# Causal attention: where the mask of the row maxima is added, which of two engines pays for it, and when the next stage's weights are loaded

## The reference

```python
# layer 0, attention, 16 heads of 16: x = x + attn(layernorm(x))
q, k, v = (jnp.einsum('bte,hed->bhtd', x, W) for W in (Wq, Wk, Wv))
scores = jnp.where(causal, jnp.einsum('bhtd,bhsd->bhts', q, k), -jnp.inf) / sqrt(E)
out = jnp.einsum('bhts,bhsd->bhtd', jax.nn.softmax(scores, axis=-1), v)
# layer 0, ffn: x = x + mlp(n) + experts(n), n = layernorm(x)
# top-k over product keys, 1024 experts (Wq, keys, down_embed, up_embed), and a gated MLP (Wg, Wu, Wd)
# layer 1: rotary attention and a mixture of experts, not touched
```

## Time and profile before

| | |
|---|---|
| time, median of 3 runs | 4173.62 us (4170.66 to 4175.27) |
| profiled execution: its own time | 4178.98 us |
| profiled execution: span | 4177.1 us |
| causal attention | from the start to about 1165 us |
| steps with m units | up to about 1120 us |
| PE busy in the span | 3942.8 us (94%) |
| DVE busy in the span | 2784.8 us (67%) |
| ACT busy in the span | 2640.7 us (63%) |

### The profile page before, as it was taken

One profiled execution on the slowest core, in us unless ns is written; L12 is line 12 of the kernel. 1 busy time (PEld: TensorE's weight loads), 2 busy tenths in 40 slices (PEclk: granted clock), 3 DMA queues, 4 the chain that ended last, 5 costly groups with the idle time before them and its releaser, 6 DMA issues. The chain is left out here.

```text
span 4177.1 us, 65914 instructions
## 1 busy us (share of the span) xinstructions
PE 3942.8 (94%) x23476; PEld 2362.2 (57%) x23476; DVE 2784.8 (67%) x5635; ACT 2640.7 (63%) x3262; POOL 1554.6 (37%) x1303
## 2 busy tenths in 40 slices
PE   7999999999968999999999989997999999999999
PEld 4455445554447788787887855554444444444444
DVE  7888778887668878878788545445545555554553
ACT  2566666666765545545455334444888888888888
POOL 3222222222334534435344211111555455455545
PEclk7999999999989999999999999999999999999999
DMA  7553444344142232332323210004666766667674
GB/s 180 129 113 75 103 99 104 91 112 111 29 121 76 61 106 77 80 103 61 109 74 84 84 35 1 1 1 106 154 154 154 163 146 154 154 148 159 148 160 99
DMA packets 205761, 429.98 MB, mean 103 GB/s; under 512 B 47584, under 2 KB 72560, under 8 KB 189056
## 3 DMA queue, kind: packets, MB, share of 16 engines
q1 hardware_dynamic: 193360, 411.56, 41.1%
q0 software_dynamic: 4160, 6.35, 0.6%
q10 hardware_dynamic: 7920, 7.87, 0.6%
HBM read 338.59 MB, written 87.03 MB: 102 GB/s over the span
## 5 line engine op out<-in xcount | busy, mean ns | idle before, releaser
L2202 ACT ACTIVATE gelu_out<-hidden,b_col 128x1024 f32<-128x1024 f32 x1024 | 1054.4, 1117 | 181.7 <-PE hidden L2125 176.0
L2185 POOL TENSOR_TENSOR combined<-combined,gated 128x512 f32<-128x512 f32 x480 | 621.5, 1295 | 647.4 <-DVE gated L2302 471.2
L663 DVE TENSOR_REDUCE maxima<-front_and_scoresT 128x1 f32<-128x512 f32 (+3 forms) x1280 | 725.6, 628 | 97.2 <-PE front_and_scoresT L471 61.7
L563 ACT ACTIVATE probsT<-front_and_scoresT 128x1024 f32<-128x1024 f32 (+3 forms) x768 | 599.4, 812 | 236.0 <-PE front_and_scoresT L498 229.8
L1127 POOL TENSOR_TENSOR pair_sums<-sims 128x1024 f32<-128x1024 f32 x256 | 482.9, 1902 | 668.3 <-DVEq L1259 412.5
L2302 DVE SCALAR_TENSOR_TENSOR gated<-out_bank,b_col,gates_spread 128x512 f32<-128x512 f32 x480 | 360.1, 750 | 511.5 <-PE out_bank L2133 482.6
L2125 PE MATMUL hidden<-slice_stack,w_stack 128*128 128x512 f32 x2048 | 622.9, 428 | 37.2 <-ACT gelu_out L2202 36.9
L1055 PE MATMUL dense<-xnT,dense_weights 128*128 128x512 f32 x2304 | 537.3, 395 | 12.7 <-ACT silu_down L1161 8.6
L2125 PEld LDWEIGHTS hidden<-slice_stack,w_stack 128*128 128x128 f32 x2048 | 354.5, 190 | 326.9 <-ACT gelu_out L2202 250.6
L2133 PE MATMUL out_bank<-gelu_out,w_sb 128*32 128x512 f32 x4096 | 517.5, 608 | 2.4 <-DVE combined L2302 2.2
L1055 PEld LDWEIGHTS dense<-xnT,dense_weights 128*128 128x128 f32 x2304 | 435.2, 190 | 112.8 <-ACT silu_down L1161 9.0
(11 more groups left out here) (205 smaller groups left out, 5063.3 us busy)
## 6 DMA issues: line engine op xcount, KB each, us to landing
gates_spread<-gate_scratch SPq DMA_DIRECT2D x512, 256.0 KB, 5.5
dense_weights<-dense_scratch SPq DMA_DIRECT2D x384, 256.0 KB, 2.8
stack_scratch<-split_parts SPq DMA_DIRECT2D x192, 256.0 KB, 3.2
slice_stack<-slice_scratch SPq DMA_DIRECT2D x128, 256.0 KB, 8.2
q_stack<-stack_scratch SPq DMA_DIRECT2D x64, 384.0 KB, 6.3
k_stack<-stack_scratch SPq DMA_DIRECT2D x64, 384.0 KB, 9.2
slice_scratch<-slice_parts SPq DMA_DIRECT2D x32, 512.0 KB, 5.9
out_x<-x_tiles ACTq DMA_DIRECT2D x15, 512.0 KB, 2.9
```

Source lines behind the costliest of these rows:

```text
L563: nc.scalar.activation(PT[:, i % NPT, 2 * pr:2 * pr + 2, at:BANK], R[:, low:high + 1:high - low, at:BANK], ACT.Exp, scale=SCALE).then_inc( ...
L663: nc.vector.tensor_reduce(dst, bank(k)[:, 0:parts * w].rearrange("p (a k) -> p a k", a=parts), AX.X, ALU.max)\
L2185: nc.gpsimd.tensor_tensor(CM[:, par, hc, :], CM[:, par, hc, :], Y[:, u % 2, :], ALU.add)\
L2202: nc.scalar.activation(GH[:, k % GHB, :, :], HP[k % HPB][:, :, :], ACT.Gelu, bias=b1c[:, n % E:n % E + 1])\
```

## The change

Four things are done.

1. The two mask matmuls are gone. For a masked block, VectorE runs one `tensor_tensor_reduce` that adds a bfloat16 mask held in SBUF to the scores in PSUM, writes the sum back to PSUM and keeps the maximum. A block left of the diagonal keeps its `tensor_reduce`. An m unit with two blocks now has two such instructions, where one reduction served both.
2. The strings of letters are new. They hold the same units as before in each step.
3. The statistics of the batches 5 to 7 are made two tiles at a time after the o units 12 to 23. The scales of the last group of batches are begun after o unit 25 and ended after 29 (before: 22 and 25).
4. `Wq`, `keys` and `down_embed` are loaded in the last step, over the buffers of the attention's weights and its transposed input, which are free by then. `ln_scales` of this stage has no block of its own any more: its first part stands ahead of the weight preparation on DVE, its second in the middle of it. `up_embed` takes the buffer of `down_embed` and is loaded once that has been transposed.

```diff
             def score_rows(k, n, g, pr, i, e):
...
-                    mm = nc.tensor.matmul(bank(k)[:, a * w:at], QS[rows, hf, q, qt * P:(qt + 1) * P],
-                                          KS[rows, hf, q, kc * BANK:kc * BANK + w], start=True, stop=not diag,
+                    mm = nc.tensor.matmul(bank(k)[:, a * w:(a + 1) * w], QS[rows, hf, q, qt * P:(qt + 1) * P],
+                                          KS[rows, hf, q, kc * BANK:kc * BANK + w], start=True, stop=True,
                                           tile_position=(64 * e, 0))
-                    if diag:
-                        nc.tensor.matmul(bank(k)[:, at - P:at], IH[half, 0, :], MH[half, :], start=False, stop=False,
-                                         tile_position=(64 * e, 0))
-                        mm = nc.tensor.matmul(bank(k)[:, at - 64:at], IH[half, 1, :], MH[half, 0:64], start=False,
-                                              stop=True, tile_position=(64 * e, 0))
...
             def row_max(k, n, g, pr, i, e):
...
-                dst = M2[:, h, at[0]:at[-1] + 1:max(at[-1] - at[0], 1)]
-                nc.vector.tensor_reduce(dst, bank(k)[:, 0:parts * w].rearrange("p (a k) -> p a k", a=parts), AX.X, ALU.max)\
-                  .then_inc(freed[False], 1)
+                for a, (qt, kc) in enumerate(MAXB[i]):
+                    part, dst = bank(k)[:, a * w:(a + 1) * w], M2[:, h, 2 * qt + kc:2 * qt + kc + 1]
+                    if kc == qt // 4:
+                        op = nc.vector.tensor_tensor_reduce(out=part, in0=part, in1=MASK[:, BANK - w:BANK], scale=1.0,
+                                                            scalar=-3e38, op0=ALU.add, op1=ALU.max, accum_out=dst)
+                    else:
+                        op = nc.vector.tensor_reduce(dst, part, AX.X, ALU.max)
+                op.then_inc(freed[False], 1)
...
-    LAST = "svsssvsssvsssvsvtssvssvvssvsvssssvsssosvssvvssosvssssvsvvssosvsvssssvssvsvsovvvo"
+    LAST = "ssvvssssstvsssvsvssvssvvsssvsvsossvssssvsssvvossvsssvssosvvssvssvsvssossssvvvvvo"
...
+                if n + 2 == NS:
+                    sp.wait_ge(freed[True], NFREE[KF["w", NS - 1, 1]])
+                    early.load(sp)
...
+class EarlyWeights:
...
+    def load(self, sp):
+        Wq, keys, down = self.arrays
+        for c in range(DC):
+            sp.dma_start(self.WQ[:, c, :, :], Wq[c * P:(c + 1) * P, :].rearrange("p (s n) -> p s n", s=2))\
+              .then_inc(self.prep_in, 16)
+        for s in range(2):
+            sp.dma_start(self.KY[:, s, :, :], keys[:, :, s, :].rearrange("h k n -> k h n")).then_inc(self.prep_in, 16)
+        sp.dma_start(self.rows_of, down.rearrange("(b p) d -> p b d", p=P)).then_inc(self.down_in, 16)
...
-        STATS_AT = {3: 5, 4: 6, 5: 7}
-        LN_AT = 4 * 6
+        TILES_AT = 2
+        STATS_AT = {12 + k: 5 * KT + TILES_AT * k for k in range((B - 5) * KT // TILES_AT)}
+        LN_AT = 28
...
 def expert_weights(...):
...
             def _(sp):
-                later_loads(sp)
+                small_loads(sp)
                 for b in range(NB):
                     sp.wait_ge(copied_dve, copies(NC + b))
                     sp.dma_start(dense.scratch[b], DP[:, b, :, :, :].bitcast(F32)).then_inc(dense.down_stored, 16)
+                sp.wait_ge(filled, NC + NB)
+                up_load(sp)
...
             def _(dve):
+                ln_begin(nc, dve, STATS, MEAN, var_ready)
                 nc.vector.memset(KB[:, :, :, :], 0.0).then_inc(zeroed, 1)
...
+                ln_end(nc, dve, STATS, RS, var_ready, sd_ready)
                 for b in range(NB):
                     dve.wait_ge(high, b + 1)
```

More of the change, by code:

```diff
@@ L37, in tile_stats, with ln_begin, ln_root, ln_end @@
     nc.vector.bn_stats(STATS[:, t, :], X[:, t, :])
[L40 removed]
+def ln_begin(nc, dve, STATS, MEAN, var_ready):
+    VE, DM = STATS[:, :, 0], STATS[:, :, 3]
+    nc.vector.tensor_tensor(MEAN[:, :], STATS[:, :, 1], STATS[:, :, 4], ALU.add)
+    nc.vector.tensor_tensor(DM, STATS[:, :, 1], STATS[:, :, 4], ALU.subtract)
+    nc.vector.tensor_tensor(VE, STATS[:, :, 2], STATS[:, :, 5], ALU.add)
+    dve.drain()
+    nc.vector.tensor_scalar(MEAN[:, :], MEAN[:, :], 0.5, None, ALU.mult)
+    nc.vector.tensor_tensor(DM, DM, DM, ALU.mult)
+    nc.vector.tensor_scalar(VE, VE, 1.0 / D, EPS, ALU.mult, ALU.add)
+    dve.drain()
+    nc.vector.scalar_tensor_tensor(out=VE, in0=DM, scalar=0.25, in1=VE, op0=ALU.mult, op1=ALU.add).then_inc(var_ready, 1)
+def ln_root(nc, act, STATS, var_ready, sd_ready):
+    act.wait_ge(var_ready, 1)
+    nc.scalar.activation(STATS[:, :, 1], STATS[:, :, 0], ACT.Sqrt).then_inc(sd_ready, 1)
+def ln_end(nc, dve, STATS, RS, var_ready, sd_ready):
+    VE, SD, R0, R1 = (STATS[:, :, i] for i in (0, 1, 4, 2))
+    dve.wait_ge(sd_ready, 1)
+    dve.wait_ge(var_ready, 1)
+    nc.vector.reciprocal(R0, SD)
+    dve.drain()
+    nc.vector.tensor_tensor(R1, R0, R0, ALU.mult)
+    dve.drain()
+    nc.vector.tensor_tensor(R1, R1, VE, ALU.mult)
+    dve.drain()
+    nc.vector.tensor_scalar(R1, R1, -0.5, 1.5, ALU.mult, ALU.add)
+    dve.drain()
+    nc.vector.tensor_tensor(RS[:, :], R0, R1, ALU.mult)
+def ln_scales(nc, STATS, MEAN, RS, tag, loads=None):
     with ExitStack() as ctx:
[L45 removed]
         var_ready = ctx.enter_context(nc.semaphore(f"var_ready_{tag}"))
```

175 lines of the change are left out of this document (74 added, 101 removed).

## The result

The changed kernel takes 4217.44 us (median of 4 runs, 4208.24 to 4224.95), the kernel before beside it 4174.44 (4170.66 to 4185.74): ratio 1.0109, interval [1.0078, 1.014]. It is 1.1% slower, where 4122 us were forecast. The profiled execution has a span of 4218.5 us.

The account below looks back on a forecast made before the run. PE was taken as the pace, busy 969 of 1005 us in the attention, with DVE close behind. Masks 41, statistics 5 and seam 6 us summed to 52 us off the median 4173.62, giving 4122 us, range 4082 to 4190.

Parts of the forecast that it names:

- The new strings can shift waits, but they can't take them away: Attention: reordered units only shift waits, since PE and DVE would both be near 90% busy; no cost was counted.
- Mask matmuls off PE: Attention: removing 1024 mask matmuls takes 82 us off PE, of which 41 us come out of the time.
- my half of 82: Attention: half of the PE time freed from masks, 41 us, was let out as gain; ends 82 and nothing.
- the dear masks: Attention, units with two blocks of 256: a mask read as 0.15 us from the timeline, 0.11 taken for 512 blocks.
- The fused maximum on DVE: Attention: fused blocks cost 0.21 to 0.61 us for 128 to 512 columns, adding 27 us to DVE.
- The rival of the dearer instruction: Attention: each fused instruction costs 70 ns more, 72 us more on DVE, still faster at 4149 us; chance 0.16.
- The read of the accumulator: DVE: the read that writes out each maximum lasts 83 ns but takes about 0.01 us of the stream.
- The rival in which DVE becomes the bound: Attention: lost overlap and reads add some 150 ns per masked block, DVE at 95%, slower at 4220 us; chance 0.14.
- Statistics in twos: Attention: splitting three bursts of batch statistics into pairs saves 5 us, between 0 and 11.
- The seam: Between attention and the next stage: earlier loads and moved scales save 6 us, bounds 3 and 8.
- The gain does not surface: Attention: freed mask time reappears as PE waits for maxima, leaving about 6 us of gain, 4168 us; chance 0.12.
- the surfacing: Attention: DVE at about 88 to 90% and a stretch 40 to 50 us shorter would prove the mask gain came out.

Follow-up runs that it names:

- e1: The changed kernel with the strings of letters of the kernel before: 4149.56 us, ratio 0.9943.
- e7: e1 with the fourth p of ODD moved from letter 60 to 92: 4214.2 us, ratio 1.0077.
- e17: The changed kernel with the transfers of maxima among a step's last p units issued by GpSimd, not SP: 4174.02 us, ratio 0.9981.
- e3: The kernel before without the two mask matmuls, the maximum taken of unmasked scores: 4140.25 us, ratio 0.991.
- e4: The kernel before with the fused maximum on DVE in place of the mask matmuls, nothing else changed: 4166.38 us, ratio 0.9969.
- e6: e4 plus the statistics in twos: 4159.89 us, ratio 0.9946.
- e2: The kernel before with only the new strings of letters: 4263.7 us, ratio 1.021.
- e12: e1 with the fourth p of ODD moved from letter 60 to 72: 4171.33 us, ratio 0.9977.
- e5: The changed kernel with ODD's third and fourth p and EVEN's last x and four p moved to earlier letters: 4206.45 us, ratio 1.0061.
- e9: e5 with the EVEN string of the kernel before: 4194.28 us, ratio 1.003.
- e10: e1 with the new ODD string: 4192.99 us, ratio 1.0021.
- e11: e1 with the new EVEN string: 4204.09 us, ratio 1.0052.
- e13: The changed kernel with the transfers of maxima among a step's last p units put behind the stack loads on SP: 4247.87 us, ratio 1.0158.
- e8: e1 with unmasked row maxima, one plain reduction per unit, in place of the fused maximum: 4127.83 us, ratio 0.9876.
- e16: e1 with two small transfers and their waits put on SP ahead of each step's stack loads: 4188.16 us, ratio 1.0017.
- e18: e11 with the transfers of maxima among a step's last p units issued by GpSimd: 4189.48 us, ratio 1.0013.
- e14: e11 with the transfers of maxima among a step's last p units put behind the stack loads on SP: 4201.94 us, ratio 1.0053.

## Why the prediction was wrong

**The step that failed** is the sentence "The new strings can shift waits, but they can't take them away". I read it only as a limit to the gain and left the strings out of the sum, at nothing. They cost 68 us (e1 against the changed kernel), more than all the rest gains. What I should have priced was in hand: the order of SP's transfers between the last p and the loads, and the distance from the fourth p to the first m that needs it: 87 units in the old ODD and 45 in the new, and in EVEN 46 and 44, but there with all four p within 13 units where they had been spread over 45. The distance by itself is not the price: e7 has the same 45 and no more waits than e1, and the old EVEN has 46. I priced every instruction that was added and nothing of what had changed places. Of the 68 us, 43 are shown to come from the transfers of maxima that stand on SP ahead of the stack loads (e17). What is left over e1 is 24 us of time, with 28 us of waits for `k_stack` still above e1's 19.5. In the trace of e17 they lie mainly behind the EVEN steps, and the ODD steps are the long ones (501.8 us against 478.0; EVEN 394.6 against 402.7). They can hold the rest, and so can the second way to lose, since the changed ODD has its fourth p at the letter of e7. No run took either away by itself.

**Mask matmuls off PE**: right in the sum, by luck. e3 gives back 40 us of time (4180.59 to 4140.25), and my half of 82 was 41. But PE's busy time in the attention falls by 58 us, not by 82; first the kernel before, then e3, each to its last add:

```profile
45.00:1164.40 1119.40, 1078.32 (x9300) 560.68 (x9300) 896.67 (x1784) 702.70 (x1044) 261.37 (x448) 0.96 0.42 98
```

```profile
45.00:1129.40 1084.40, 1020.50 (x7252) 484.19 (x7252) 894.82 (x1786) 701.92 (x1044) 261.51 (x448) 0.96 0.44 101
```

So the price was too high and the part that comes out too low: some two thirds, where DVE's work stays the same. I had read the dear masks, 0.15 us, from 603.66 to 604.53, but at 604.23 an s matmul starts in that stretch as well.

**The fused maximum on DVE**: mis-sized. I subtracted 80 ns of overlap and priced 0.61 us for 512 columns; the next one starts 0.65 us behind [600.30 and 600.95 above]. The durations are 323, 457, 584 and 724 ns, against my 285, 415, 550 and 690: each block is 34 to 42 ns dearer, whatever its size: a fixed part that no row of before has. DVE's work in the attention grew by 58 us (896.7 to 955.1), not by 27. On the path that is 26 us (e4 against e3). So fused and matmuls together give 14 us, where I had 41. The rival of the dearer instruction put +70 ns on a block and 4149 us on the whole; with the old order the time is 4149.56, but with half that price on a block, so the match is luck too.

**The read of the accumulator** lasts 140 ns, not 83, but the next instruction starts at the same 600.30: it costs nothing, as in the earlier trace rows. The rival in which DVE becomes the bound is refuted, also by its own sign: DVE is at 85% above, and at 89% in e1, whose window is:

```profile
45.00:1050.00 1005.00, 950.18 (x6523) 450.46 (x6523) 893.54 (x2865) 630.19 (x933) 228.75 (x392) 0.95 0.46 107
```

The kernel ended on its side, 4217 against its 4220 us, by another mechanism. The Trainium skill, "VectorE: DVE Perf Modes", section "The DRAIN you can't avoid", would have the next operation wait for an empty pipe, but adds that one that is not held starts earlier. The trace shows the earlier start for the fused operation too, 0.73 us long and 0.65 us apart.

**Statistics in twos**: 6.5 us (e4 to e6, 4166.38 to 4159.89), forecast 5. The two intervals overlap, so the size is rough. The sign came true at the first burst: in e4 it starts at 344.20 and the clock from 343 to 357 us is 0.76, in e6 it is 1.00 there. The changed kernel has 0.75 us where the earlier trace rows had 2.71:

```profile
341.26 0.75 DVE L37 BATCH_NORM_STATS2 ln_stats<-x_tiles 128x6 f32<-128x256 f32 x2
```

**The seam**: 7.3 us in the traces (10.8 to 3.5), forecast 6. The medians of e6 and e1 differ by 10 us and their ratios by 1, so the total times only bound it. The traces say more: from the last add to the end of the span the kernels with the old seam (before, e2, e3, e4, e6) need 3011 to 3012 us, those with the new one 3005 to 3009, but for e17 with 3011.5. That is 3 to 7 us. The second part of the scales runs beside the transposes as foretold (L63 at 1217.79).

**The gain does not surface**: this rival holds for a part of the gain. The waits for maxima are 208 us in e1 as well (75.9, 64.6, 43.1 and 24.3 for s and m), against 147 before. In e3, where nothing took the masks' place, they are 181: 34 us more, in which a part of the mask time that went from PE came back. The other 26 or so came with the fused maximum (e4: 207). They are the same in both orders, so they are not the 68 us. DVE at 89% did not prove the surfacing, as I had said it would: e1 has it, and its attention is 12 us shorter, not 40 to 50.

With the old order the whole is a gain of 24 to 31 us against 52 forecast; most of that difference is in masks and maximum together, 14 us where I had 41.

(The lower end of my own range, 4090, does not follow from its sum: all of the 82 and the 11 give 4081. Nothing rests on it.)

**What stays open**: why e12 loses 22 us (14 by the ratios) by moving one p 12 letters, how much of e5's and e9's loss is the place of p among x, w and o, and what costs e10 the 28 us that its waits don't hold. DVE's stop at such a p is seen, and that e7 and e12 differ by 43 us. But the stop of PE in e7 is 1.83 us and its ODD steps are 6.2 us longer each, so it explains a part at most; no run moved a p without moving its neighbours' banks too.

## What to carry to other kernels

An order of instructions that is written by hand is a schedule for the DMA queue too: before changing it, list for every load what stands in its queue between its last producer and itself, and the distance to its first user. Look for the loss in the step that was changed (e7) and in the one behind it (e10, e11). A wait that is taken away by a swap in the same queue goes to the other side of the swap (e13); only another queue took it away (e17), and the cheapest way to less work was not to do it (e8).

## What the runs showed of the hardware

- A stall of PE for a load cost 1.0 to 1.7 times its length in e16 to e18. Behind a wait of 6.84 us (e11) four matmuls took 3.78 instead of 1.98 us, and the stretch of 13 us around it had a mean granted clock of 0.61.
- The fused add and maximum with PSUM in and out takes 323 ns for 128 columns and 724 for 512, starts every 0.65 us at 512, and its read of 140 ns starts together with the next instruction.
- A 32 KB store behind four 384 KB loads in the same queue ended after 9.1 us (e14); 3.4 us is the median of such stores in the changed kernel.
